# Two heads of an attention unit set half a unit apart on one Trainium2 core

## The reference, cut to what matters

```python
q = jnp.einsum('bnd,de->bne', ln, Wq)                    # queries from x: 1024
kv_in = jnp.concatenate([xn, ln], axis=1)                # context (77), then x (1024)
k, v = jnp.split(jnp.einsum('bnd,de->bne', kv_in, Wkv), 2, axis=-1)
sim = jnp.einsum('bhid,bhjd->bhij', q * scale, k)        # 1024 x 1101, head width 64
sim = jnp.where(full_mask[:, None, None, :], sim, max_neg)
out = jnp.einsum('bhij,bhjd->bhid', jax.nn.softmax(sim, axis=-1), v)
out = jnp.einsum('bne,ed->bnd', out, Wout)
return layer_norm(out, g_o, b_o)
```

## Time and profile before

| | |
|---|---|
| median of 3 runs | 2089.75 us (2084.55 to 2089.76) |
| the profiled execution | 2084.4 us, span 2082.6 us |
| busy share of the span | PE 92%, DVE 69%, ACT 47%, POOL 36% |
| stage 6, first to last exponential | 1099.6 to 1968.4 us: 869 us, 128 units |

### The profile page before, as it was taken

How to read it: one execution, slowest core, us unless ns; L and a number is a source line. 1 busy time by engine, 2 the same in 40 slices (tenths; PEclk the granted TensorE clock), 3 DMA queues, 4 the chain that set the end, 5 groups by cost and what they waited for, 6 DMA issues and landing times.

```text
span 2082.6 us, 33216 instructions
## 1 busy us (share of the span) xinstructions
PE 1921.5 (92%) x11797; PEld 1355.2 (65%) x11797; DVE 1435.7 (69%) x2676; ACT 978.5 (47%) x2079; POOL 752.3 (36%) x1145
## 2 busy tenths in 40 slices
PE   6997799696999988997878999999999999998999
PEld 3885799542699976883565666666675666655644
DVE  5775111467344457787867999999878999998755
ACT  5672333343111252226875555555545555555455
POOL 1002111000522200000006777777656777777500
PEclk9897899898999999998989999999999999999999
DMA  3702899502489960002002333333222333333201
GB/s 115 208 2 79 273 323 333 170 1 86 163 292 321 310 228 1 1 1 86 1 13 60 82 83 82 83 83 83 72 57 72 82 82 82 82 82 81 63 1 41
DMA packets 191184, 226.87 MB, mean 109 GB/s; under 512 B 28939, under 2 KB 167085, under 8 KB 191021
## 3 DMA queue, kind: packets, MB, share of 16 engines
q1 hardware_dynamic: 183725, 201.98, 33.0%
q0 software_dynamic: 7296, 22.78, 3.3%
HBM read 127.64 MB, written 29.91 MB: 76 GB/s over the span
## 4 chain that ended last, share of the span: by engine, by line
PE 45%; ACT 6%; DVE 3%; issue 1%; POOL 0%; ACTq 0%; DVEq 0%; POOLq 0%
PE ps L640 41%; ACT w_odd L1796 4%; PE ps L1214 2%; PE ps L1215 1%; ACT arena L1785 1%; PE ps L1106 0%; DVE w_odd L2532 0%; DVE small L2410 0%; POOL arena L1908 0%; ACT out_feat L1708 0%; PE ps L1115 0%; ACT xn_tok L1651 0%; DVE small L2522 0%; ACT out_feat L1714 0%; DVE arena L2380 0%
## 5 line engine op out<-in xcount | busy, mean ns | idle before, releaser
L1908 POOL COPY arena<-w_odd 32x512 f32<-32x512 f32 x1024 | 623.7, 609 | 254.4 <-DVE w_odd L2532 202.1
L640 PE MATMUL ps<-arena,w_odd 128*128 128x128 f32 (+4 forms) x2352 | 468.2, 441 | 3.0 <-DVE arena L2202 1.2
L640 PE MATMUL ps<-arena 128*64 128x256 f32 (+4 forms) x3248 | 392.3, 370 | 8.3 <-DVE arena L2333 4.4
L640 PEld LDWEIGHTS ps<-arena 128*64 128x64 f32 (+4 forms) x3248 | 258.9, 155 | 119.5 <-issue 22.6
L2532 DVE STREAM_TRANSPOSE w_odd<-w_odd 128x1024 f32<-128x1024 f32 x256 | 317.4, 1245 | 14.6 <-ACT w_odd L1796 3.0
L1796 ACT ACTIVATE w_odd<-ps,small 128x1101 f32<-128x1101 f32 x256 | 301.6, 1179 | 48.0 <-DVE small L2522 41.0
L640 PEld LDWEIGHTS ps<-arena,w_odd 128*128 128x128 f32 (+3 forms) x2352 | 286.3, 188 | 27.9 <-issue 18.7
L1781 ACT ACTIVATE arena<-ps 77x256 f32<-77x256 f32 x128 | 48.5, 379 | 295.4 <-PE ps L1215 295.4
L2522 DVE TENSOR_REDUCE small<-ps 128x1 f32<-128x1101 f32 x128 | 166.9, 1304 | 29.3 <-PE ps L640 28.1
L1893 POOL DMA_INDIRECT token_rows<-arena x62 | 59.8, 964 | 292.3 <-DVE arena L2223 292.3
L2523 DVE TENSOR_REDUCE small<-ps 128x1 f32<-128x1024 f32 x128 | 155.4, 1214 | 0.0
(11 more groups left out here) (398 smaller groups left out, 2909.8 us busy)
## 6 DMA issues: line engine op xcount, KB each, us to landing
arena<-w_odd SPq DMA_DIRECT2D x1024, 64.0 KB
w_odd<-in_s_w SPq DMA_DIRECT2D x32, 1024.0 KB, 7.4
w_odd<-in_s_wgu SPq DMA_DIRECT2D x30, 704.0 KB, 6.1
w_even<-in_s_w SPq DMA_DIRECT2D x15, 1024.0 KB, 7.3
arena<-expert_rows_in SPq DMA_DIRECT2D x62, 130.0 KB, 4.7
w_odd<-in_s_wd SPq DMA_DIRECT2D x30, 256.0 KB, 3.6
out_feat<-in_s_wgu SPq DMA_DIRECT2D x10, 704.0 KB, 5.9
expert_rows_in<-zero_row POOLq DMA_DIRECT2D x1, 5070.0 KB, 33.2
```

Source lines behind the costliest of these rows:

```text
L640: return pe.matmul(o, lhsT, rhs, start=start, stop=stop, **kw)
L1908: pool.tensor_copy(s6_d[u % 4][32 * j:32 * j + 32, :, 256 * i:256 * i + 256], s6_pm[u % 2][32 * i:32 * i + 32, :, 256 * j:256 * j + 256]). ...
```

## The change

In each unit the heads are taken one after the other, half a unit apart. Head 0 gets PSUM banks 0 to 2 and head 1 banks 3 to 5, so two banks (6 and 7) are left for everything else. `scores(u, h)` makes the scores of one head; so that both row halves of the array still work beside each other, the head's 1024 keys from x are split over the halves (`s6_k` is laid out anew, made by matmuls of 64 output columns), and the queries are kept a second time with the halves swapped (`s6_qs`), which SP makes with two DMAs per new query piece. The mask enters as one more matmul of 77 columns against rows of ones, in place of DVE's addition. Each head waits only for its own exponential. `weigh` is cut in two around the second head's scores and stands in even units, the pieces in odd ones. The reciprocals are spread by an ACT copy (`s6_rb`) and two transposes on PE in place of four matmuls. DVE takes one maximum of 1101 columns per head.

```diff
-        s6_q = [cut(WO, 6016 + 1024 * i, S) for i in range(2)]
+        s6_q, s6_qs = cut(WO, 6016, S), cut(WO, 7040, S)
...
+        s6_k = [cut(AR, 9216 + 1024 * i, 2, 512) for i in range(2)]
...
+        s6_sc = [psf[:, 0:KV], psf[:, 6 * 512 - KV:6 * 512]]
+        s6_cs = [psf[:, S:KV], psf[:, 6 * 512 - KV:6 * 512 - S]]
...
+        def pieces_of(u):
+
+            n, j = divmod(u, 8)
+            own = [("w", n, 0)] if j == 1 and 1 <= n < 16 else []
+            return own + [("w", n + 1, i) for i in (j - 1, j) if j % 2 and i and n < 15]
...
-            return 5 + r6_no[key] % 3
+            return 6 + r6_no[key] % 2
...
+            def swapped(lo, hi):
+
+                for r in (0, 64):
+                    sp.dma_start(s6_qs[64 - r:P - r, lo:hi], s6_q[r:r + 64, lo:hi]).then_inc(q6_in, 16)
+
+            sp.wait_ge(c6_sb, 8)
+            swapped(0, S)
+            turns = 1
             for u in range(NU):
+                for key in pieces_of(u):
+                    kind, lo, hi = PIECES[key[2]]
+                    if kind == "q":
+                        copied(sp, key)
+                        sp.wait_ge(q6_in, 32 * turns)
+                        swapped(lo, hi)
+                        turns += 1
...
+                        w0 = c * P + 64 * (kind == "k1")
                         for k in range(KD):
-                            rhs = XNT[:, k, b * S:(b + 1) * S]
-                            if kind == "q":
-                                rhs = rhs[:, lo:hi]
-                            else:
-                                rhs = rhs.rearrange("p (i a n) -> p a i n", a=4, i=8)[:, lo // 256:hi // 256]
-                            last = mm(PS[:, bank, 0:hi - lo], w[:, k, c * P:(c + 1) * P], rhs, start=(k == 0), stop=(k == 1))
+                            keys = XNT[:, k, b * S:(b + 1) * S].rearrange("p (i a n) -> p a i n", a=4, i=8)
+                            for half in range(2):
+                                rhs = keys[:, 2 * half + lo // 256:2 * half + hi // 256]
+                                last = mm(PS[64 * half:64 * half + 64, bank, 0:hi - lo], s6_wk[:, k, w0:w0 + 64], rhs, start=(k == 0), stop=(k == 1))
...
-                    if t >= 3:
-                        copied(pe, r6_keys[t - 3])
+                    if t >= 2:
+                        copied(pe, r6_keys[t - 2])
...
-                def scores(u):
+                def scores(u, h):
 
                     n, qt = divmod(u, 8)
-                    if qt == 0 and n == 0:
+                    if u == 0 and h == 0:
                         pe.wait_ge(c6_sb, 8)
-                    elif qt == 0:
-                        copied(pe, ("w", n, 6))
-                        copied(pe, ("w", n, 7))
+                    if h == 0 and qt == 0:
+                        pe.wait_ge(q6_in, 32 * max(1, 2 * n))
+                        if n:
+                            copied(pe, ("w", n, 7))
+                    elif h == 0 and qt == 4 and n:
+                        pe.wait_ge(q6_in, 32 * (2 * n + 1))
                     if u:
-                        pe.wait_ge(a6_p, 2 * u)
+                        pe.wait_ge(a6_p, 2 * u - 1 + h)
+                    own, other = 64 * h, 64 - 64 * h
                     q0 = qt * P
-                    def tokens(h, i):
-                        r = 64 * h
-                        return mm(PS[:, 3 * h + i, :], s6_q[n % 2][r:r + 64, q0:q0 + P], s6_k[n % 2][r:r + 64, i * 512:(i + 1) * 512])
-
-                    def context(h):
-                        r = 64 * h
-                        return mm(s6_both[:, h], s6_q[n % 2][r:r + 64, q0:q0 + P], s6_kx[n % 2][r:r + 64])
-
-                    context(0).then_inc(a6_s, 1)
-                    tokens(1, 0)
-                    tokens(0, 0).then_inc(a6_s, 1)
-                    pe.wait_ge(a6_s, 4 * u + 1)
-                    context(1).then_inc(a6_s, 1)
-                    tokens(0, 1)
-                    tokens(1, 1).then_inc(a6_s, 1)
+
+                    def tokens(r):
+                        q = s6_q if r == own else s6_qs
+                        return mm(PS[:, 4 * h + r // 64, :], q[r:r + 64, q0:q0 + P], s6_k[n % 2][r:r + 64, h])
+
+                    mm(s6_cs[h], ones[other:other + 64], s6_mk[other:other + 64, n // 8], stop=False).then_inc(a6_m, 1)
+                    tokens(own).then_inc(a6_s, 1)
+                    tokens(other).then_inc(a6_s, 1)
+                    pe.wait_ge(a6_m, 2 * u + h + 1)
+                    mm(s6_cs[h], s6_q[own:own + 64, q0:q0 + P], s6_kx[n % 2][own:own + 64], start=False).then_inc(a6_s, 1)
...
-                    pe.wait_ge(a6_rb, g + 1)
+                    pe.wait_ge(r6_bc, g + 1)
                     bank = free_bank(("r", g))
                     for i in range(2):
-                        for h in range(2):
-                            r = 64 * h
-                            last = mm(PS[r:r + 64, bank, i * P:(i + 1) * P], s6_rc[:, g % 2, 2 * i + h:2 * i + h + 1].broadcast_to([P, DH]), ident[:, :])
+                        last = pe.transpose(PS[:, bank, i * P:(i + 1) * P], s6_rb[g % 2][:, 2 * i:2 * i + 2].rearrange("p a b -> p (a b)"), ident[:, :])
...
-                        scores(u)
+                        scores(u, 0)
+                    if not even:
+                        for key in pieces_of(u):
+                            piece(key[1], key[2], free_bank(key)).then_inc(r6_mm, 1)
+                    elif 4 <= u < NU + 4:
+                        weigh((u - 4) // 2, 0, 5)
+                    if 1 <= u <= NU:
+                        ctx_turn(u - 1)
+                    if u < NU:
+                        scores(u, 1)
...
+                    if even and 4 <= u < NU + 4:
+                        weigh((u - 4) // 2, 5, NKT)
                     if not even and 3 <= u < NU + 3:
-                        weigh((u - 3) // 2)
-                    if even and u >= 4 and (u // 2 - 2) % 32 >= 28:
-                        project(u // 2 - 2)
+                        sums_turn((u - 3) // 2)
+                    if not even and u >= 5 and (u - 5) // 2 % 32 >= 28:
+                        project((u - 5) // 2)
...
+                        act.wait_ge(a6_rb, g + 1)
+                        if g >= 2:
+                            act.wait_ge(r6_mm, r6_no["r", g - 2] + 1)
+                        act.activation(s6_rb[g % 2], s6_rc[:, g % 2].unsqueeze(2).broadcast_to([P, 4, DH]), ACT.Copy).then_inc(r6_bc, 1)
...
+                    if not even:
+                        for key in pieces_of(u):
+                            piece(key[1], key[2], filled(key)).then_inc(r6_act, 1)
...
+                    if u < NU:
+                        if u >= 2:
+                            moved(act, u - 2)
+                        exponential(u, 0)
+                    if 1 <= u <= NU:
+                        context_copy(u - 1)
...
+                def turn(u, h):
+
+                    dve.wait_ge(a6_p, 2 * u + h + 1)
+                    dve.transpose(s6_pm[u % 2][:, h], s6_pm[u % 2][:, h]).then_inc(t6_done, 1)
...
+                    if 1 <= u <= NU:
+                        if even:
+                            g = (u - 2) // 2
+                            if g >= 2:
+                                dve.wait_ge(r6_bc, g - 1)
+                            dve.wait_ge(a6_p, 2 * u)
+                            dve.reciprocal(s6_rc[:, g % 2], s6_sm[:, g % 2]).then_inc(a6_rb, 1)
+                        turn(u - 1, 1)
                     if u < NU:
                         for h in range(2):
-                            dve.wait_ge(a6_p, 2 * u + h + 1)
-                            dve.transpose(s6_pm[u % 2][:, h], s6_pm[u % 2][:, h]).then_inc(t6_done, 1)
-                        if not even:
-                            g = u // 2
-                            if g >= 2:
-                                dve.wait_ge(r6_mm, r6_no["r", g - 2] + 1)
-                            dve.reciprocal(s6_rc[:, g % 2], s6_sm[:, g % 2]).then_inc(a6_rb, 1)
-                    if even and u >= 6 and 28 <= (u // 2 - 3) % 32 < 31:
-                        added(u // 2 - 3)
-                    if even and u >= 4 and (u // 2 - 2) % 32 >= 28:
-                        normed(u // 2 - 2)
-                    if not even and u >= 5 and ((u - 1) // 2 - 2) % 32 == 31:
-                        added((u - 1) // 2 - 2)
+                            dve.wait_ge(a6_s, 6 * u + 3 * h + 3)
+                            dve.tensor_reduce(s6_nm[:, u % 2, h:h + 1], s6_sc[h], AX.X, ALU.max, negate=True).then_inc(a6_mx, 1)
...
+                    if u < NU:
+                        turn(u, 0)
```

More of the change, by code:

```diff
@@ L219, in build @@
         s6_ptc = [cut(AR, 8192 + 512 * i, 2, 2 * P, rows=C) for i in range(2)]
-        s6_k = [cut(AR, 9216 + 1024 * i, S) for i in range(2)]
+        s6_k = [cut(AR, 9216 + 1024 * i, 2, 512) for i in range(2)]
         s6_v = [cut(AR, 11264 + 1152 * i, NKT, P) for i in range(2)]
         s6_r = [cut(AR, 13568 + 256 * i, 2 * P) for i in range(2)]
```

(66 more changed lines are left out.)

93 lines of the change are left out of this document (40 added, 53 removed).

## The result

| | before | after |
|---|---|---|
| median of the runs | 2088.15 us (2084.55 to 2089.76, 4 runs) | 2150.56 us (2149.45 to 2152.8, 4 runs) |
| the profiled execution | 2084.4 us | 2152.8 us |
| PE busy | 1921.5 us | 1978.4 us |

The changed kernel is slower: ratio 1.0303, 95% interval 1.0284 to 1.0321. I had forecast 2136 (2104 to 2158), slower with a chance of 0.91.

A forecast was written before the change was run, and what follows sets the result against it. PE's own work was taken to bound stage 6: +58 work, -10 waits, +3 chain, +4 start = +55, less 2 clock and 2 tail, about +51 on 2084.4, so 2135; median 2136 us (2104 to 2158).

The forecast's parts named there:

- PE's own work sets the stage: Stage 6: PE busy 414.66 of 418.40 us over 65 steady units, so the amount of its work counts, not the order.
- A half block of scores costs 1.28: Scores of one head on PE: 1.28 us, two heads 2.56 against 2.14 before; +0.42 per unit, +54 us over 128 units.
- Of it 0.13 per unit for the mask: Scores on PE: 0.13 of the +0.42 us per unit is mask columns, the rest opening a block twice.
- Weigh in two, +10; key pieces, +7; sums, -13: PE's work: one more weigh block +10 us, tile shape changes in key pieces +7, two transposes for the sums -13.
- The start waits 4 us for the swap: Stage start: PE's first scores wait for two 256 KB DMAs of swapped queries, +4 us, nothing hidden.
- -2 for the clock: Near the end: one half-clock stretch behind the long waits may go, -2 us.
- The chain costs +3 in the odd units: Odd units with long pieces: head 0's exponential comes 0.1 us late for PE's next scores, 32 x 0.1 = +3 us.
- the chain becomes the bound: Rival: piece copies or DVE's transposes come 0.6 us later, odd units wait 0.7; +32 more, 2168 us; chance 0.13.
- the other three: Rivals on score blocks: openings at half price, 2110, chance 0.12; at no price, 2084, 0.09; halves serial, 2190, 0.03.
- no-price rival: Each half block of scores: weights load beside the block before, so the second opening costs nothing; median 2084 us; chance 0.09.
- Waits: -10: Stage 6: 18 us of PE's waits for exponentials go, 8 come back (unit 123: 2; context copy's bank: 6).
- -2 in the tail: Kernel's tail: weigh stands behind a projection, which hides its last waits, -2 us.

The follow-up runs named there:

- b_cut: The kernel before with only its scores cut in two, ctx_turn(u-1) standing in the middle; 2160.04 us, ratio 1.0356 to the kernel before.
- c_back: The changed kernel reordered: both heads' scores back to back, weigh whole, ACT's piece copies behind both exponentials; 2127.08 us, ratio 1.0125 to the kernel before.
- c_back_d: The back-to-back reordering of the changed kernel, with the mask on DVE and each head's context scores first; 2106.49 us, ratio 1.0031 to the kernel before.
- a_dmask: The changed kernel with the mask added by DVE per head in place of a matmul; 2152.17 us, ratio 1.0320 to the kernel before.
- a_ncopy: The changed kernel with ACT's copy of the stage 7 row transposes moved ahead of its unit's second exponential; 2146.04 us, ratio 1.0287 to the kernel before.
- b_sums: The kernel before with the new sums alone: ACT copy and two transposes in place of four matmuls; 2081.87 us, ratio 0.9977 to the kernel before.

## Why the prediction was right, point by point

- *PE's own work sets the stage, not the exponentials that its weight loads waited for.* Right: the waits for exponentials fell by 10 us and the kernel got slower; PE is busy 378.25 of 378.25 us. The work grew by 54 us for the forecast's +58, and by about 52 without the clock.
- *A half block of scores costs 1.28.* Right: 1.276 as the median of 237 blocks. b_cut shows the cause, since the cut alone gives it; c_back and c_back_d show the way back.
- *Of it 0.13 per unit for the mask.* This split was wrong: b_cut has no mask and pays the same 1.276 per half, and a_dmask gives 0.045 per head, 0.09 per unit, for taking the mask away. The total did not hang on it: it came from whole blocks of the trace.
- *Weigh in two, +10; key pieces, +7; sums, -13.* Worked out from the traces: 0.15 x 64 = +10, about 0.3 per eight units or +5, and 0.216 x 64 = -14.
- *The start waits 4 us for the swap.* 4.85, where 0.52 stood before. That PE's clock would fall behind this wait was not in the sum: it had -2 for the clock, by one stretch less near the end, and about +2 came, since two of three half-clock stretches at the start last 6.8 us each.
- *The chain costs +3 in the odd units.* It cost nothing: a head's exponential was ready in time in all steady units. The rival that the chain becomes the bound is out; so are the other three by the 1.276. (The sum of the no-price rival, 4 - 10 + 4, is -2 and not -4; at 2082 in place of 2080 it changes nothing here.)
- *Waits: -10, +3 and +4 for the start, -2 in the tail, together -5.* This term was wrong in sign and makes nearly all of the 14.6 us by which the median lies above 2136: PE's idle time in the stage grew by 10.5, 15.5 more than forecast. I had 6 us in sixteen units for the context copy's bank, and these waits came as 5.5 (L1802). What I had missed is the next user of the two banks, weigh. It waits for the copy of the row transposes, 0.71 and 1.07 by turns, 7.1 in all (L1816), and behind the projection's output, which DVE holds through its statistics, about 1.0 five times and 2.3 once, 7.1 in all (L2525). a_ncopy took the first 7.1 away, and the profiled execution became shorter by 7.4.
- *2135 for the profiled execution, 2136 for the median.* 2152.8 and 2150.56. Some of the difference is chance: the profiled execution is the highest of the four here, and before it lay below all four (2084.4 against 2084.55 to 2089.76).

## What to carry to other kernels

Where PE is busy nearly without a gap, an order that removes its waits can win little (19.9 us here), and every cut that it needs costs. Price each cut of a matmul block by what it opens and by the columns that then stand alone on one half (here 0.41 us for scores, both together; 0.15 for weigh; 0.15 for two transposes), and put blocks of one tile shape side by side. Read PE's waits from the matmuls and not from the weight loads. Count the banks that a new buffer takes from the rotation, and who then waits for which copy; the parts of the change that only saved work (the transposed sums, maxima of one piece, head 0's scores finished first) made the fastest kernel once they were put in the old order, with the mask on DVE; of them only the sums were also tried alone (0.9977).

## What the hardware showed that I had not expected

- A weight load runs ahead of its matmul only where the tile shape stays. In b_sums the first load of ctx_turn, behind 64-row score tiles, starts together with its matmul; the load of the sums, behind tiles of its own shape, starts 0.10 us ahead:

```profile
1411.15 0.14 PEld L1216 LDWEIGHTS ps<-ident,w_odd 128*77 128x77 f32 x1 [0.76 <-issue]
1411.15 0.33 PE L1216 MATMUL ps<-ident,w_odd 128*77 128x128 f32 x1
...
1411.33 0.26 PEld L1224 LDWEIGHTS ps<-ident,arena 128*128 128x128 f32 x2
1411.43 0.38 PE L1224 MATMUL ps<-ident,arena 128*128 128x128 f32 x2
```

  The changed kernel's steady units show the same at the openings of its score blocks. So the mechanism that the no-price rival named, first weights loaded beside the block before, does not come about there. How much of an opening is this load and how much something else, no run here separates.
- The price of a change of tile shape is plain in two transposes: 0.22 us with blocks of their own shape on both sides, 0.27 with one change (c_back_d, the fence above), 0.37 with two, between blocks of scores. The Trainium skill, "TensorEngine Tiling (Array Packing)", Key Properties, says that a change of mode drains the engine; the trace agrees that each change costs time, and 0.15 is what the two cost here.
- Matmuls on different row halves seem to start out of program order: the second pass of the context scores starts at 1421.52, and the first 512-column pass on the other half, of a later matmul, at 1421.36. The Trainium skill, "TensorE: Matmul & The Clock Gate", The mechanism, has a strict order of starts; the trace disagrees if the two passes of a matmul stand next to each other in PE's instructions, which it doesn't show.
- The kernel before took 2086.9 to 2088.2 us (medians) beside most of these kernels and 2099.67 beside c_back and c_back_d: 0.6% between chips, more than some of the effects above.
